# Reordered weight loads and norm sums in a hand-scheduled attention and expert kernel

## The reference

```python
x = x + xattn(layernorm(x), ctx)        # relu(q) relu(k), scores, relu(scores / sqrt(512) + mask), times relu(v), relu
x = x + ffn(layernorm(x))               # x and weight rounded to an FP6 grid in blocks of 32, then x @ w.T + bias
x = x + mix(layernorm(x), ctx)          # x @ W1.T + mean of ctx @ W2.T + b
x = x + experts(layernorm(x))           # below
logits = x @ Wg + bg                    # 16 experts
probs  = softmax over the 2048 rows of a batch; each expert takes its 128 best rows
h = relu(tok @ w1 + b1); h = relu(h @ w2 + b2); out = (h @ w3 + b3) * vals; scatter-add at the rows
```

## Time and profile before

| | us |
|---|---|
| median of 3 runs | 795.95 |
| lowest and highest | 795.36, 796.16 |
| profiled execution | 794.5 |
| its span | 792.7 |

### The profile page before, as it was taken

The page is one execution under the profiler, slowest core; times in us unless marked ns, Lnnn a source line. Parts: engine busy times, 40 slices in busy tenths (PEclk is TensorE's granted clock), DMA queues, the critical chain, the costliest instruction groups (busy, mean ns, idle before and its releaser), DMA issues.

```text
span 792.7 us, 12071 instructions
## 1 busy us (share of the span) xinstructions
PE 721.0 (91%) x4100; PEld 591.3 (75%) x4100; DVE 542.7 (68%) x1000; ACT 451.1 (57%) x807; POOL 429.0 (54%) x596
## 2 busy tenths in 40 slices
PE   6999999999999998998867598759999999999993
PEld 6766888888888887786756244324699999999993
DVE  5787579787787989989879698100356667666751
ACT  5754676777777777566454263213456666666540
POOL 2735788888888887677555270501314443333231
PEclk9999999999999999999999699979999999999997
DMA  9600121212212221111442688799348888877643
GB/s 310 227 28 14 41 94 67 94 58 93 67 57 94 80 82 41 55 41 55 147 154 78 224 287 271 222 355 276 76 149 247 245 235 236 239 239 233 190 84 50
DMA packets 60446, 115.61 MB, mean 146 GB/s; under 512 B 5601, under 2 KB 6881, under 8 KB 60385
## 3 DMA queue, kind: packets, MB, share of 16 engines
q1 hardware_dynamic: 53216, 98.05, 37.2%
q0 software_dynamic: 7168, 16.78, 9.7%
HBM read 89.26 MB, written 25.17 MB: 144 GB/s over the span
## 4 chain that ended last, share of the span: by engine, by line
issue 25%; PE 19%; DVE 18%; DMA 15%; POOL 10%; ACT 10%; SPq 1%; POOLq 0%; ACTq 0%; DVEq 0%
DMA out<-y,ids 12%; PE bank L931 6%; PE bank L282 6%; POOL rstd_all L1900 3%; ACT xn L1096 2%; DVE bn L1397 2%; DVE left L1623 2%; PE bank L289 2%; DVE pos L1617 2%; DVE pack L1613 2%; DVE x L1560 2%; POOL x L1987 1%; DMA stage<-wq 1%; ACT qT_h L1155 1%; POOL xd L1979 1%
## 5 line engine op out<-in xcount | busy, mean ns | idle before, releaser
L2022 POOL DMA_INDIRECT out<-y,ids x24 | 56.2, 2341 | 131.4 <-DVE y L1844 127.7
L931 PE MATMUL bank<-gap_w,gap_xT 128*128 128x512 f32 x192 | 92.2, 622 | 12.3 <-issue 10.8
L1409 DVE TENSOR_TENSOR w_l<-w_raw,w_h 128x2048 fp32r<-128x2048 f32 x33 | 75.6, 2290 | 26.5 <-ACT w_h L1040 26.5
L1342 ACT ACTIVATE h<-bank,b 128x512 f32<-128x512 f32 x48 | 33.0, 687 | 80.3 <-PE bank L282 80.3
L931 PEld LDWEIGHTS bank<-gap_w,gap_xT 128*128 128x128 f32 x192 | 35.9, 199 | 49.0 <-issue 46.1
L1409 DVE TENSOR_TENSOR hT_l<-h,hT_h 128x512 fp32r<-128x512 f32 x48 | 33.2, 691 | 50.9 <-ACT hT_h L1348 49.4
L1040 ACT ACTIVATE w_h<-w_raw 128x2048 fp32r<-128x2048 f32 x33 | 62.2, 1925 | 0.0
L282 PE MATMUL bank<-wf_h,xdT_h 128*128 128x512 f32 x128 | 53.2, 416 | 5.8 <-DVE xdT_l L1409 5.8
L282 PE MATMUL bank<-hT_h,w_h 128*128 128x256 f32 x192 | 54.3, 283 | 1.4 <-DVE hT_l L1409 1.4
L1409 DVE TENSOR_TENSOR tokT_l<-bank,tokT_h 128x512 fp32r<-128x512 f32 x24 | 15.4, 684 | 57.7 <-ACT tokT_h L1040 57.7
L282 PE MATMUL bank<-tokT_h,w_h 128*128 128x256 f32 x192 | 54.7, 285 | 0.0
(11 more groups left out here) (273 smaller groups left out, 2435.7 us busy)
## 6 DMA issues: line engine op xcount, KB each, us to landing
w_raw<-w SPq DMA_DIRECT2D x36, 1024.0 KB
gap_w<-w SPq DMA_DIRECT2D x24, 1024.0 KB, 6.3
x<-x SPq DMA_DIRECT2D x32, 256.0 KB, 2.8
out<-x SPq DMA_DIRECT2D x32, 256.0 KB, 2.1
xn<-xn SPq DMA_DIRECT2D x32, 256.0 KB, 2.0
mask<-mask_t SPq DMA_DIRECT2D x8, 256.0 KB, 3.1
stage<-wk SPq DMA_DIRECT2D x1, 1024.0 KB, 8.8
stage<-wq SPq DMA_DIRECT2D x2, 512.0 KB, 8.8
```

Of the source, the lines that this page charges most:

```text
L931: last = pe.matmul(ps[4 + s][:, :], gx[s][:, d * P:(d + 1) * P], gw[n % 4][:, d, :], start=(d == 0), stop=(d == C - 1))
L1342: act.activation(h32[n % 2][:, :], ps_hid[n % 4][:, :], ACT.Relu, bias=bias)
L1409: dve.tensor_tensor(dst, src, hi_part, ALU.subtract).then_inc(sem, 1)
L2022: pool.indirect_dma_start(out=out_rows, out_offset=bass.IndirectOffsetOnAxis(ap=ids[:, r:r + 1], axis=0), in_=y[e % 2][b][:, :], in_offset ...
```

## The change

1. SyncE's list: gap loads 14 to 17 now come ahead of w_raw loads 3 to 5, and gap loads 18 to 20 alternate with those.
2. `sums3(j)` moves from the end of ScalarE's turn j+1 into turn j+2, and `rstd_of(2, j)` on GpSimd from the end of turn j+1 to the end of turn j+2 (in turn 32 further ahead).
3. `late_bias(k)` is true where `quant_first(k)` is, and in turns 20 to 31 altogether. In those turns GpSimd's mix bias comes behind xd, and rstd3 behind the ffn bias; so does `s_lo` behind rstd3 in turns 23 and 27.
4. `logit_parts(g)` for g = 0 to 6 runs on GpSimd at the end of its turn; VectorE's `logit_scale` waits for it by a new semaphore `g_lg`. The last group stays on VectorE.
5. The last tile's `norm4` and its store come behind the last logits' row and store.
6. The counts of top-k steps per turn become 6, 5, 5, 5, 5, 5, 4, 5, 3, 3, 2 for turns 20 to 30; they were 6, 5, 4, 5, 5, 5, 3, 5, 4, 3, 3.

```diff
@@ -342,6 +342,10 @@
     LAST_SUMS = N - 2
     THIRD = range(19, 31)
 
+    def late_bias(k):
+
+        return quant_first(k) or 20 <= k < N
+
     def third_stats(eng, j):
 
         if j in THIRD:
@@ -353,7 +357,7 @@
 
     def steps_of(k):
 
-        first = {20: 0, 21: 6, 22: 11, 23: 15, 24: 20, 25: 25, 26: 30, 27: 33, 28: 38, 29: 42, 30: 45, 31: STEPS}
+        first = {20: 0, 21: 6, 22: 11, 23: 16, 24: 21, 25: 26, 26: 31, 27: 35, 28: 40, 29: 43, 30: 46, 31: STEPS}
         return range(first[k], first[k + 1]) if 20 <= k < 31 else []
 
     def rows_of(b):
@@ -523,6 +527,11 @@
             sp.wait_ge(sm.p_s, G)
             sp.dma_start(cand[b][:, :, :], pack[rows_of(b), :]).then_inc(sm.k_cand, 16)
 
+        def store_xn4(j):
+
+            sp.wait_ge(sm.a_xn4, j + 1)
+            sp.dma_start(xn4_tiles[j], xn4[j % 2][:, :]).then_inc(sem_xn4[j % 2], 16)
+
         for k in range(0, LAST + 1):
             if k + XR < N:
                 load_x(k + XR)
@@ -537,13 +546,14 @@
             if valid(j):
                 sp.wait_ge(sm.d_x3, j + 1)
                 sp.dma_start(out_tiles[j], x3[j % 2][:, :]).then_inc(sem_x3[j % 2], 16)
-                sp.wait_ge(sm.a_xn4, j + 1)
-                sp.dma_start(xn4_tiles[j], xn4[j % 2][:, :]).then_inc(sem_xn4[j % 2], 16)
+                if j < N - 1:
+                    store_xn4(j)
             g = logits_of(k)
             if g is not None:
                 sp.wait_ge(sm.a_seg, g + 1)
                 first = g // GB * E * GB + g % GB
                 sp.dma_start(seg[first:first + (E - 1) * GB + 1:GB, :], lrow[g % 2][:, :]).then_inc(sem_seg[g % 2], 16)
+        store_xn4(N - 1)
 
         def load_raw(i):
             e, layer = order[i]
@@ -562,9 +572,12 @@
         for n in range(10, 14):
             load_gap(n)
         sp.wait_ge(sem_gtok[1], 16 * 3)
+        for n in range(14, 18):
+            load_gap(n)
         for i in range(RAW, 2 * RAW):
             load_raw(i)
-        for n in range(14, GAP):
+            load_gap(18 + i - RAW)
+        for n in range(21, GAP):
             load_gap(n)
         for i in range(2 * RAW, len(order)):
             load_raw(i)
@@ -1218,6 +1231,8 @@
                 act.wait_ge(sm.p_t3, j + 1)
                 act.wait_ge(sm.p_c, max(0, j - 1))
                 hi(sm.a_hi3, x2T[j % 2][0][:, :, :], in4(ps_ta))
+            if k - 2 in THIRD and quant_first(k):
+                sums3(k - 2)
             j = k - 3
             if valid(j):
                 act.wait_ge(sm.d_x3, j + 1)
@@ -1240,7 +1255,9 @@
             j = k + 9
             if valid(j) and k >= 1:
                 hi1(j)
-            if valid(k - 3) and not quant_first(k):
+            if k - 2 in THIRD and not quant_first(k):
+                sums3(k - 2)
+            if valid(k - 3) and not quant_first(k) and k - 3 != N - 1:
                 norm4(k - 3)
             g = scores_of(k)
             if g is not None:
@@ -1255,11 +1272,9 @@
                 act.wait_ge(sm.p_t2, j + 1)
                 act.wait_ge(sm.p_f, j)
                 hi(sm.a_hi2, xd_h[:, :, :], in4(ps_tb))
-            if valid(k - 3) and quant_first(k):
+            if valid(k - 3) and quant_first(k) and k - 3 != N - 1:
                 norm4(k - 3)
-            if k - 1 in THIRD:
-                sums3(k - 1)
-            if k == 21:
+            if k == 22:
                 exp_rows(0, vbias)
             if k == 0:
                 setup("v1")
@@ -1284,6 +1299,7 @@
                     act.wait_ge(sem_seg[g % 2], 16 * (g // 2))
                 act.activation(lrow[g % 2][:, :], ps_ta[0:E * GRP, 0:P], ACT.Identity, bias=bg[:, 0:1])\
                     .then_inc(sm.a_seg, 1)
+        norm4(N - 1)
 
         phase1_over(act)
 
@@ -1547,6 +1563,8 @@
 
             dve.wait_ge(sm.g_r4, GRP * (g + 1))
             dve.wait_ge(sm.p_seg, g)
+            if g < G - 1:
+                dve.wait_ge(sm.g_lg, g + 1)
             four = slice(GRP * g, GRP * (g + 1))
             dve.tensor_tensor(lg_t[:, :].rearrange("p (e a) -> p a e", a=GRP), lg[:, :, :],
                               r_all[1][:, four].unsqueeze(2).to_broadcast([P, GRP, E]), ALU.mult).then_inc(sm.d_lg, 1)
@@ -1776,8 +1794,8 @@
             j = k + 10
             if valid(j) and k >= 2 and j < FIRST_SUMS:
                 stats1(j)
-            if parts_of(k) is not None:
-                logit_parts(parts_of(k))
+            if parts_of(k) == G - 1:
+                logit_parts(G - 1)
             if not ahead(k):
                 for n in steps_of(k):
                     top_step(0, n)
@@ -1964,12 +1982,29 @@
                 pool.wait_ge(sm.a_set, A["row1"])
             pool.tensor_tensor(x2[j % 2][:, :], x2[j % 2][:, :], cbias[:, batch(j), :], ALU.add).then_inc(sm.g_x2b, 1)
 
+        def logit_parts(g):
+
+            pool.wait_ge(sm.a_l, GRP * (g + 1))
+            pool.wait_ge(sm.g_r3, GRP * (g + 1))
+            pool.wait_ge(sm.d_lg, g)
+            if g % GB == 0:
+                pool.wait_ge(sm.d_set, V["cg"])
+            four = slice(GRP * g, GRP * (g + 1))
+            both = lt[g % 2]
+            then(pool.tensor_tensor(lg_sum[:, :, :], both[:, :, 0:2 * E], both[:, :, 2 * E:4 * E], ALU.add))
+            then(pool.tensor_tensor(lg[:, :, :], lg_sum[:, :, E:2 * E],
+                                    r_all[0][:, four].unsqueeze(2).to_broadcast([P, GRP, E]), ALU.mult))
+            then(pool.tensor_tensor(lg[:, :, :], lg[:, :, :], lg_sum[:, :, 0:E], ALU.add))
+            pool.tensor_tensor(lg[:, :, :], lg[:, :, :],
+                               cgrow[:, g // GB, :].unsqueeze(1).to_broadcast([P, GRP, E]), ALU.add)\
+                .then_inc(sm.g_lg, 1)
+
         for k in range(LAST + 1):
             if valid(k):
                 rstd_of(1, k, sm.d_st2, sm.g_r2)
-            if valid(k - 2) and k != 2 and not quant_first(k):
+            if valid(k - 2) and k != 2 and not late_bias(k):
                 mix_bias(k - 2)
-            if valid(k - 3) and not quant_first(k):
+            if valid(k - 3) and not late_bias(k):
                 rstd_of(3, k - 3, sm.d_st4, sm.g_r4)
             if valid(k):
                 pool.wait_ge(sm.d_xs, k + 1)
@@ -1978,19 +2013,23 @@
                 pool.wait_ge(sm.p_t2, k)
                 pool.tensor_tensor(blocks(xd[:, :]), blocks(q8[:, :]), spread(xs64[:, :], NB), ALU.mult)\
                     .then_inc(sm.g_xd, 1)
-            if valid(k - 2) and quant_first(k):
+            if valid(k - 2) and late_bias(k):
                 mix_bias(k - 2)
             if valid(k):
                 pool.wait_ge(sm.a_xc, k + 1)
                 if k == 0:
                     pool.wait_ge(sm.c_late, LATE)
                 pool.tensor_tensor(x1[k % 2][:, :], x1[k % 2][:, :], fbias[:, :], ALU.add).then_inc(sm.g_x1b, 1)
-            if valid(k - 3) and quant_first(k):
+            g = scores_of(k)
+            if valid(k - 3) and late_bias(k):
                 rstd_of(3, k - 3, sm.d_st4, sm.g_r4)
+            if g is not None and late_bias(k):
+                s_lo(g)
+            if k == N:
+                rstd_of(2, N - 2, sm.d_st3, sm.g_r3)
             if valid(k - 1) and k - 1 not in THIRD:
                 rstd_of(2, k - 1, sm.d_st3, sm.g_r3)
-            g = scores_of(k)
-            if g is not None:
+            if g is not None and not late_bias(k):
                 s_lo(g)
             if valid(k + 10):
                 rstd1(k + 10)
@@ -2000,8 +2039,11 @@
                 q_lo(*unit)
             if k == 2:
                 mix_bias(0)
-            if k - 1 in THIRD:
-                rstd_of(2, k - 1, sm.d_st3, sm.g_r3)
+            if k - 2 in THIRD and k != N:
+                rstd_of(2, k - 2, sm.d_st3, sm.g_r3)
+            g = parts_of(k)
+            if g is not None and g < G - 1:
+                logit_parts(g)
 
 
         def gather(e):
```

More of the change, by code:

```diff
@@ L70, in build @@
         a_sum a_st1 a_st4 a_xn1 a_xc a_xn4 a_hi1 a_hi2 a_hi3 a_q a_s a_l a_seg
-        g_r1 g_r2 g_r3 g_r4 g_b4 g_x1b g_xd g_qlo g_x2b s_lo
+        g_lg g_r1 g_r2 g_r3 g_r4 g_b4 g_x1b g_xd g_qlo g_x2b s_lo
         a_st3 k_top k_cand k_exp k_idx k_tr k_out k_pos a_soft
```

## The result

The changed kernel takes 802.98 us (median of 4 runs, 801.46 to 803.45) against 795.65 for the kernel before: a ratio of 1.0090, with an interval of 1.0072 to 1.0107. It is slower by 7.3 us. The forecast was 794.5, with a range of 787 to 800.5; the time lies above the range.

The account below looks back on a forecast made before the run. Bounds: TensorE to turn 19, VectorE, then a ScalarE-VectorE-GpSimd loop, VectorE's second top-k list, layer 14's weight wait, then TensorE. Terms -11.6 + 3.2 + 7.4 - 0.4 = -1.4 us on 795.95 gave 794.5, range 787 to 800.5.

Parts of the forecast that it names:

- part 1: Small-expert (gap) layers: the new weight-load order removes layer 14's wait of 10.83 us and its cold clock; -11.6 us.
- ring: Turns 20 to 24 and 27: late rstd3 delays normalisation, xdT_h, xdT_l and next xc serially; turns 20 to 24 +9.5 us.
- part 5: End of phase 1: with the last logits ahead of the normalisation and xn store, TensorE's transpose leads; -0.4 us.
- By layer 20 ... about 9.2 MB must have landed: Gap layers: at 383 GB/s the loads need 24.0 us against 23.4 available; 0.9 us charged with the hops.
- R4: Gap layers: the weight wait returns at layer 20 or 21, at 304 GB/s; 802.2 us, chance 0.14.
- Part 2: Turns 6, 10, 14, 18: logit sums on GpSimd delay second-layernorm scalars, s_l and attend; 0.8 us each, +3.2 us.
- R1: The logit sums moved to GpSimd are hidden in its idle time; 789.1 us, chance 0.20.
- Part 3: Turns 20 to 27: bias adds and rstd3 behind dequantising; +9.5 for 20 to 24, -0.4 for 25 and 26, +4.1 for 27.
- R3: Turns 20 to 23: TensorE idles and half-clock stretches join the ring; 797.9 us with two, 801.3 with four; chance 0.20.
- R2: Turns 20 to 31: the ring never closes and VectorE goes on as before; 781.1 us, chance 0.08.
- Part 4: Turns 28 to 30: sums made a turn later lie in a wait; 26.3 us against 32.4, -6.1 us.
- The xn store lands within the logits' 3.48 us: End of phase 1: the xn store, now issued behind the logits' store, adds no landing time beyond the logits' own.

Follow-up runs that it names:

- e9: The changed kernel measured again with no edit: 801.81 us.
- e1: The kernel before with only the new order of weight loads: 788.39 us.
- e6: The kernel before with w_raw loads 3 to 5 behind all gap loads: 782.46 us.
- e13: The changed kernel with w_raw loads 3 to 5 behind all gap loads: 797.27 us.
- e12: The kernel before with the edits of e3, e6 and e10 together, plus the logit sums of group 4 alone on GpSimd: 771.39 us.
- e4: The kernel before with only the logit sums of groups 0 to 6 moved to GpSimd: 798.18 us.
- e2: The changed kernel with ScalarE's norm4 of turns 20 to 24 and 27 put behind the copy xdT_h: 786.88 us.
- e3: The kernel before with the third layernorm's sums and scalars a turn later only in turns that quantise first: 789.03 us.
- e7: The kernel before with only the last tile's norm4 and store put behind the last logits' row and store: 796.48 us.
- e8: As e7, and VectorE does not wait for the xn stores at the end of phase 1: 796.04 us.
- e10: As e8, with VectorE's copy of the first batch's values behind top-k step 8 instead of 5: 794.50 us.
- e14: As e12, with the values' copy behind top-k step 14 and gap load 14 ahead of the wait for the token gather: 771.22 us.

## Why the prediction was wrong

The largest miss is one term: part 1, forecast -11.6 and measured -5.0 in the profiled execution, -7.1 in e9's and -7.5 alone (e1). The rest is a ring sized 2.5 us short (3.8 in e9) and the wrong sign of part 5. Part 6, the counts of top-k steps, was not run by itself.

**Part 1.** The stall at layer 14 went, as said, and the cold clock behind it. The step that failed is "By layer 20 ... about 9.2 MB must have landed". That sum runs from the end of layer 13 (TensorE free, load 17 issued, at 527.22) to the landing of load 20 (557.18). The window (columns as in the earlier trace rows):

```profile
527.22:557.18 29.96, 23.91 (x72) 10.84 (x70) 0.00 (x0) 8.58 (x13) 4.56 (x4) 1.00 1.05 374
```

and its two large queues, q1 with SyncE's loads and q0 with GpSimd's gathers and scatters (packets, MB, share):

```profile
q1 hardware_dynamic: 4686, 9.30, 83.7%
q0 software_dynamic: 706, 1.87, 21.1%
```

It took 30.0 us, where I had 24.0, and 11.2 MB moved. The rate, 374 GB/s against 383, costs 0.7 us of that; the other 5.2 are 2.0 MB that I didn't count. The seven loads that I counted (17 to 20 and w_raw 3 to 5, which are in the list up to load 20) are right. But about 1.0 MB of loads 21 to 23, issued behind load 20, had also moved when it landed: 2.13 of their 3.15 MB came after it. And the rest of loads 15 and 16, the token gathers and the scatters made 2.8 MB, of which I estimated 1.9. 10.5 to 17.5 us passed from issue to landing for loads 15 to 22. Rival R4 had the event (a return of the wait, 802.2 us) at 0.14, and laid it to a lower rate; the layer was 19 and 20 instead of 20 or 21. That its 802.2 lies so near the measured 802.98 is luck, since the other parts missed too. That the place of the w_raw loads is the cause is shown by e6 and e13: with them last no wait for weights over 0.5 us is left (in e12 one of 1.54 us, at layer 16). What stays open is why one execution waited 5.8 us and others, with the same list, about 2. In e9 10.2 MB moved in the same stretch, 1.0 less.

**Part 2.** Right: forecast +3.2, measured +2.6 between xc of turn 0 and of turn 20, and +2.8 there in e4. (e4's +2.3 for the whole program is a sum with other signs in it.) The step was the one named, later s_l: the waits for s_l before turn 20, by the view of that tile, before and after (who waited, us, times):

```profile
  PEld bank L282: 1.5, 4
```

```profile
  PEld bank L282: 4.6, 4
  PE bank L282: 3.6, 4
```

The weight loads waited 3.1 us longer in all. R1, that it would be hidden, falls. The remark on turn 22 was right in kind and small in size: four VectorE operations and not one product were freed, 3.4 us in e4.

**Part 3.** The ring came as described, instruction by instruction, and its turns within 0.6 us but one: 15.0, 15.0, 14.4, 17.1 and 10.9 against 14.7, 15.0, 13.4, 16.8 and 10.4. Turn 22 took 1.0 us more. There the mix bias waits for ScalarE's sums as in turn 21, but longer, 1.57 us instead of 0.68, since the copy ahead of those sums waited for TensorE's transposes, in a stretch at a granted clock of 0.50. GpSimd's mix bias and the window of that stretch in turn 22, then the mix bias in e9:

```profile
320.45 1.28 POOL L1983 TENSOR_TENSOR x<-x,mix_bias 128x512 f32<-128x512 f32 x1 [1.57 <-ACT v_bias L1111]
```

```profile
313.80:317.00 3.20, 3.20 (x9) 2.50 (x8) 2.99 (x7) 2.27 (x6) 1.68 (x5) 0.50 0.23 84
```

```profile
320.87 1.29 POOL L1983 TENSOR_TENSOR x<-x,mix_bias 128x512 f32<-128x512 f32 x1 [2.75 <-ACT v_bias L1111]
```

In e9 and e13 the half clock in turn 22 lasts longer, this wait is 2.75 and 2.79 us, and the turn takes 15.5 and 15.6. Less what the wait exceeds 0.68, turn 22 is 13.5 us in all three, against 13.4 forecast. So R3, the half clock that joins the ring, was there: 0.9 us in the profiled execution and 2.1 in the two others, of the 3.4 it was given. R2, that the ring never closes, falls: it closed as long as norm4 stood ahead of xdT_h, and without that (e2) the time is 786.9.

**Part 4.** 26.3 us for turns 28 to 30, as forecast; in e3, without part 3, they take 26.8, and turns 25 and 26 win 1.0 us more.

**Part 5.** Forecast -0.4, measured +1.1 in e7. The failed step is "The xn store lands within the logits' 3.48 us". Phase 2 begins when both stores have landed, and the second one issued is the last one: the logits issued first landed in 1.8 us, the xn store behind them in 3.78. I took the 3.48 us for the logits' own. In e7 alone the first top-k step comes 0.7 us later after x3; the rest of the row's +1.2 lies in turn 31, which took 0.6 us longer up to x3, where I had 0.3.

The sum of the spans' difference: 2.58 + 9.60 + 1.16 - 5.03, and 0.19 from before the first xc: 8.50. My sign that layer 14 would start about 2 us before 524.1 also failed: it starts at 527.2.

## What to carry to other kernels

A load that is issued early for a later stage is not free when the DMA engines are full: it is paid by the loads that land in the same stretch. Loads issued behind the one that is waited for take their share too (1.0 MB here), so count all bytes in flight up to the deadline. Before an instruction is moved later on one engine, look for what stands behind its consumer on the next engine: here one normalisation that nobody needed stood ahead of a copy that everybody needed, and its place was worth 16 us. A gain won ahead of a chain of hand-overs is only as long as the slack at the next one (e8, e10, e14).

## What the runs showed of the hardware

- Of the last two stores of phase 1, the second one issued took 3.4 to 3.9 us to land in every profile: 32 KB of logits in 3.48 us, issued at 441.93, 0.37 us behind a 256 KB store; with the order turned round, the logits in 1.8 us and the 256 KB store in 3.78. Its place alone does not explain this: in the changed kernel the logits of turn 30, issued at 434.19, 0.36 us behind such a store, landed in 1.81 us. What the cause is stays open.
- In e1 a wait of 2.19 us was followed by a stretch at a granted clock of 0.50 (matmuls of 3.28 instead of 1.88 us), and so was one of 2.09 us in e9 (3.18 us); the waits of 3.34 and 2.48 us in the changed kernel's first profile were not (1.96 us, clock 1.00). So the length of the wait alone doesn't tell.
- Issuing itself can take long on SyncE's queue. In the changed kernel it took 2.0 to 3.4 us for each of six weight loads issued from 531.56 to 547.36, when four or five earlier ones had not landed, and 0.37 to 0.45 us for those issued with three under way, though the share of the DMA engines was about 1 all the time.
